# A four-layer graph attention stack: layers 1 and 3 start their first pass on eight source tiles with a maximum of their own, and rescale the sums later

## The reference, cut to what matters

```python
h = max(layernorm(x), 0)
Wh = h @ W;  s1 = Wh @ a1;  s2 = Wh @ a2
e = leaky_relu(s1[:, None] + s2[None, :], 0.2)
att = softmax(where(adj > 0, e, -big), axis=1)
x = x + activation(att @ Wh)     # elu, gelu in layer 1
```

## Time and profile before

| | |
|---|---|
| median of 3 runs | 751.4 us (751.36 to 753.15) |
| profiled execution | 751.58 us, its span 749.9 us |
| PE busy | 739.0 us, 99%, 6504 records |
| DVE busy | 624.9 us, 83% |
| ACT busy | 327.3 us, 44% |
| granted clock | 0.999 over the span |

### The profile page before, as it was taken

The page is one execution under the profiler, slowest core; times in us unless marked ns, Lnnn a source line. Parts: engine busy times, 40 slices in busy tenths (PEclk is TensorE's granted clock), DMA queues, the critical chain, the costliest instruction groups (busy, mean ns, idle before and its releaser), DMA issues.

```text
span 749.9 us, 16133 instructions
## 1 busy us (share of the span) xinstructions
PE 739.0 (99%) x6504; PEld 731.6 (98%) x6504; DVE 624.9 (83%) x1061; ACT 327.3 (44%) x899; POOL 16.6 (2%) x38
## 2 busy tenths in 40 slices
PE   9999999999999999999999999999999999999998
PEld 9899999999999999999999999999989989998998
DVE  5999879797797968879796797969887969797987
ACT  4978432462443336134353414534450362546230
POOL 4000000000000000000000000000000000000000
PEclk9999999999999999999999999999999999999999
DMA  9991000000000000000000000000000000000011
GB/s 294 370 386 78 30 29 1 28 0 28 28 0 28 0 28 0 28 28 0 28 0 28 28 0 28 0 0 1 30 2 1 1 29 2 1 1 29 2 29 29
DMA packets 14370, 30.98 MB, mean 41 GB/s; under 512 B 1384, under 2 KB 7680, under 8 KB 14336
## 3 DMA queue, kind: packets, MB, share of 16 engines
q1 hardware_dynamic: 11648, 21.58, 8.1%
q0 software_dynamic: 2688, 8.92, 3.5%
HBM read 29.37 MB, written 1.13 MB: 41 GB/s over the span
## 4 chain that ended last, share of the span: by engine, by line
PE 92%; DVE 3%; ACT 3%; issue 1%; POOL 0%; DVEq 0%; POOLq 0%
PE acc L514 55%; PE acc L552 24%; PE side L657 3%; PE side L458 3%; ACT adjT L805 1%; DVE probs L1433 1%; PE acc L479 1%; PE acc L607 1%; ACT V L838 1%; PE acc L437 1%; PE side L622 0%; DVE stats L1538 0%; PE side L577 0%; PE side L591 0%; PE side L489 0%
## 5 line engine op out<-in xcount | busy, mean ns | idle before, releaser
L514 PE MATMUL acc<-V,probs 128*128 128x129 f32 x3840 | 436.8, 275 | 2.0 <-DVE probs L1334 1.5
L514 PEld LDWEIGHTS acc<-V,probs 128*128 128x128 f32 x3840 | 432.7, 192 | 2.9 <-DVE V L1278 1.6
L1342 DVE SCALAR_TENSOR_TENSOR probs<-rho,t_now,adjT 128x1024 f32<-128x1024 f32 x238 | 289.9, 1277 | 10.5 <-PE acc L514 8.5
L1433 DVE SCALAR_TENSOR_TENSOR probs<-rho,t_now,adjT 128x640 f32<-128x640 f32 (+4 forms) x185 | 148.3, 857 | 15.0 <-PE acc L552 11.8
L906 ACT ACTIVATE hpT<-rows 32x256 f32<-32x256 f32 x224 | 92.8, 414 | 66.6 <-DVE rows L1379 64.2
L552 PE MATMUL acc<-stage,probs 128*128 128x129 f32 x1024 | 116.9, 275 | 0.1
L552 PEld LDWEIGHTS acc<-stage,probs 128*128 128x128 f32 x1024 | 115.4, 192 | 0.8 <-issue 0.5
L552 PE MATMUL acc<-V,probs 128*128 128x129 f32 x768 | 90.6, 276 | 0.4 <-DVE probs L1433 0.3
L552 PEld LDWEIGHTS acc<-V,probs 128*128 128x128 f32 x768 | 88.0, 192 | 1.0 <-DVE probs L1433 0.5
L891 ACT ACTIVATE fill<-mean_now,empty 128x128 f32<-128x128 f32 x120 | 36.7, 395 | 92.4 <-DVE den L1355 92.3
L1387 DVE TENSOR_TENSOR X<-X,side 128x512 f32<-128x512 f32 x28 | 19.3, 688 | 63.5 <-PE side L657 63.5
(11 more groups left out here) (213 smaller groups left out, 407.6 us busy)
## 6 DMA issues: line engine op xcount, KB each, us to landing
stage<-in_adj_t_dram SPq DMA_DIRECT2D x24, 512.0 KB, 8.0
rho<-rho_dram POOLq DMA_DIRECT2D x15, 512.0 KB, 3.9
hpT<-in_adj_t_dram SPq DMA_DIRECT2D x4, 512.0 KB, 8.7
xn<-in_adj_t_dram SPq DMA_DIRECT2D x4, 512.0 KB, 9.2
rho<-s_dram SPq DMA_DIRECT2D x3, 512.0 KB, 3.8
X<-in_x_dram SPq DMA_DIRECT2D x2, 512.0 KB, 4.4
W0t<-in_W_t_dram SPq DMA_DIRECT2D x1, 512.0 KB, 5.2
W<-in_L_gnn_W_heads_dram SPq DMA_DIRECT2D x1, 512.0 KB, 6.5
```

The costliest lines, as they stand in the source:

```text
L514: last = nc.tensor.matmul(group(c, k), probs[:, j % RING, k * P:(k + 1) * P], V[:, j, :], start=(j == 0 and k % PER_BANK == 0), stop=(j == ...
L1342: nc.vector.scalar_tensor_tensor(probs[:, j % RING, :], rho[:, c * CH:(c + 1) * CH], t_now[:, j:j + 1], adjT[:, j, c * CH:(c + 1) * CH], A ...
L1433: return nc.vector.scalar_tensor_tensor(slot_of(n, p, j)[:, first:end], rho[:, at + first:at + end], t_now[:, j:j + 1], adjT[:, j, at + fi ...
```

## The change

In layers 1 and 3 (`EARLY`) the first pass is cut in two. For source tiles 0 to 7, whose scores exist since pass 2 of the layer before, a maximum of their own is taken (`early_maximum`, spread by PE in `spread_early_max`, `early_center`). t, v and rho of their own are made (`early_factors`, `early_rho`, into a new buffer `rho_early`), V is scaled with them (`scale_early_v`), and the eight tiles of pass 0 are spread through the hole, on DVE and on PE. When the true maximum is there, ACT multiplies the sums in PSUM by a factor for each target, one bank after another (`rescale`), and then the tiles 8 to 15 are added. For passes 1 to 3 V of tiles 0 to 7 is brought to the true maximum by one more multiplication. The `keep_warm` calls of these two holes go, `late_s1` moves behind tiles 10 and 11 of pass 0, the mean of layer 3 moves to pass 1, and layer 2 keeps its form but for the order of `late_s1`.

The diff below goes from PE's order to ACT's (`factors_after_early`) and to DVE's (from `tiles(0, 2, 9, 16)` on), here for layer 1. DVE's order for layer 3 is the same in kind: the tiles 0, 1, 2 and 3 to 4 stand behind the statistics of chunk 2, behind its norm, behind the norm of chunk 3, and behind `take_scores` and `late_scale`.

```diff
+    EARLY = (1, 3)
-        spare_bank, max_bank = acc[:, 0, 2, 0:2 * P], acc[:, 0, 2, 2 * P:3 * P]
+        spare_bank, max_bank, early_bank = side[:, 0, 0:P], side[:, 0, P:2 * P], acc[:, 0, 2, 2 * P:3 * P]
+            def early_unit(n, asides):
+                for j in range(NK - 2):
+                    early_tile(n, j, range(NK))
+                    if j in asides:
+                        asides[j]()
+                for ks in banks_of():
+                    for j in (NK - 2, NK - 1):
+                        last = early_tile(n, j, ks)
+                    if ks[-1] < NK - 1:
+                        last.then_inc(early_summed, 1)
+            def rest_of_first_pass(n, asides):
+                for b, ks in enumerate(banks_of()):
+                    pe.wait_ge(rescaled, NB * (early_no(n) - 1) + b + 1)
+                    if b == 0:
+                        pe.wait_ge(late_v_ready, late_v_no(n, NK))
+                    for j in (NK, NK + 1):
+                        pe.wait_ge(probs_ready, probs_no(n, 0, j) + 1)
+                        early_tile(n, j, ks)
...
+            def spread_early_max(n):
+                pe.wait_ge(early_max_ready, early_no(n))
+                nc.tensor.matmul(early_bank, early_max[:, 0:1].to_broadcast([P, P]), ident_neg[:, :],
+                                 start=True, stop=True).then_inc(early_maxT_psum, 1)
-            def rest_of_scores(n):
...
+            def first_layer_scores():
+                project_rows(2, 0)
+                early_unit(1, {
+                    0: lambda: (transpose_normed(1, 1, 0, x_written, chunk_no(1, 1, 0)),
+                                transpose_normed(1, 1, 1, x_written, chunk_no(1, 1, 1))),
+                    1: lambda: (late_wh(1, 1, 0), transpose_rows(3, 0, hT_ready, chunk_no(1, 1, 0)), late_wh(1, 1, 1),
+                                transpose_normed(1, 2, 0, x_written, chunk_no(1, 2, 0))),
+                    2: lambda: (project_rows(3, 0), late_wh(1, 2, 0)),
+                    3: lambda: transpose_normed(1, 3, 0, x_written, chunk_no(1, 3, 0)),
+                    4: lambda: (late_wh(1, 3, 0), spread_late_max(1))})
+            def third_layer_scores():
+                early_unit(3, {
+                    0: lambda: (transpose_normed(3, 1, 1, hT_ready, chunk_no(3, 0, 1)), late_wh(3, 1, 0)),
+                    1: lambda: (late_wh(3, 1, 1), transpose_normed(3, 2, 0, x_written, chunk_no(3, 2, 0))),
+                    2: lambda: (late_wh(3, 2, 0), transpose_normed(3, 3, 0, x_written, chunk_no(3, 3, 0))),
+                    3: lambda: late_wh(3, 3, 0),
+                    4: lambda: spread_late_max(3)})
...
-                             (11, 1): lambda: rows_of_s1(1)})
+                             (11, 1): lambda: rows_of_s1(1),
+                             (13, 1): lambda: spread_early_max(1)})
...
+                    rest_of_first_pass(1, {10: lambda: late_s1(1, 3), 11: lambda: late_s1(1, 2)})
...
+                    rest_of_first_pass(3, {10: lambda: late_s1(3, 3), 11: lambda: late_s1(3, 2), 14: lambda: sum_raw(3)})
...
-                        late_unit(n, 2, {(0, 1): half[1], (4, 0): half[2], (6, 0): half[3], (13, 1): lambda: rows_of_s1(m)})
-                        late_unit(n, 3, {})
+                        late_unit(n, 2, {(0, 1): half[1], (4, 0): half[2], (6, 0): half[3], (10, 1): lambda: rows_of_s1(m),
+                                         (12, 1): lambda: spread_early_max(m)})
+                        late_unit(n, 3, {(14, 1): five[0]})
...
+                    late_unit(3, 1, {(1, 1): lambda: mean_rows(3, WL[:, 2, 0:D], 1, late_rho_ready, 12)})
...
+            def factors_after_early(n):
...
+                late_rho(n, 0)
+                late_rho(n, 1)
+                act.wait_ge(factor_ready, e)
+                rescale(n, 0)
+                act.wait_ge(late_vexp_ready, n)
+                scale_late_v(n, 8, 12)
+                rescale(n, 1)
+                rescale(n, 2)
+                scale_late_v(n, 12, 16)
+                nc.scalar.activation(v[:, 0:NK, :], v[:, 0:NK, :], ACT.Copy, scale=shift[:, 1:2]).then_inc(v_rescaled, 1)
+                late_rho(n, 3)
+                late_rho(n, 2)
...
-            tiles(0, 2, 9, 16)
-            take_scores(1, 0)
+            tiles(0, 2, 9, 13)
+            early_maximum(1)
+            tiles(0, 2, 13, 16)
+            early_center(1)
             add_to_x(1, 1, 0)
             add_to_x(1, 1, 1)
             late_statistics(1, 1)
             late_denominators(1, 2)
             late_divide(1, 2, 0)
             late_scale(1, 1)
             late_elu_rows(2, 0)
             late_norm(1, 1)
+            tiles(1, 0, 0, 1)
             late_denominators(1, 3)
             late_divide(1, 3, 0)
             add_to_x(1, 2, 0)
             late_elu_rows(3, 0)
+            tiles(1, 0, 1, 2)
             late_statistics(1, 2)
             late_norm(1, 2)
+            tiles(1, 0, 2, 3)
             add_to_x(1, 3, 0)
             late_statistics(1, 3)
             late_norm(1, 3)
+            tiles(1, 0, 3, 4)
             take_scores(1, 1)
             late_scale(1, 2)
+            tiles(1, 0, 4, 5)
...
                 take_scores(n, 2)
+                if n in EARLY:
+                    tiles(n, 0, 5, 6)
+                    late_center(n)
+                    tiles(n, 0, 6, 7)
+                    rescale_factors(n)
+                    late_vy(n)
+                    tiles(n, 0, 7, 16)
+                    tiles(n, 1, 0, 6)
+                    if n > 1:
+                        mean(n, n)
...
-                    tiles(3, 1, 8, 13)
+                    tiles(3, 1, 8, 10)
+                    mean_elu(3)
+                    tiles(3, 1, 10, 13)
+                    add_fill(3)
                     add_linear(4, 0, 0)
                     add_to_x(4, 0, 0)
                     tiles(3, 1, 13, 14)
```

More of the change, by code:

```diff
@@ L527, in last_bank_read, with banks_of, early_tile @@
                     pe.wait_ge(late_rows, rows_no(n, p, i))
+            def banks_of():
+                return [range(b * PER_BANK, min((b + 1) * PER_BANK, NK)) for b in range(NB)]
+            def early_tile(n, j, ks):
+                if j in (0, 1, 4) and ks[0] == 0:
+                    pe.wait_ge(early_v_ready, 3 * early_no(n) - 2 + (0, 1, 4).index(j))
+                if j < NK:
+                    pe.wait_ge(probs_ready, probs_no(n, 0, j) + 1)
+                for k in ks:
+                    last = nc.tensor.matmul(late_group(0, k), slot_of(n, 0, j)[:, k * P:(k + 1) * P], V_of[n % 2][:, j, :],
+                                            start=(j == 0 and opens_bank(0, k)), stop=(j == NT - 1), skip_group_check=True)
+                if ks[-1] == NK - 1:
+                    last.then_inc(summed, 1)
+                return last
+            def early_unit(n, asides):
[14 more added lines that the diff above has]
+                    for j in (NK, NK + 1):
+                        pe.wait_ge(probs_ready, probs_no(n, 0, j) + 1)
+                        early_tile(n, j, ks)
+                for j in range(NK + 2, NT):
+                    if j == 12:
+                        pe.wait_ge(late_v_ready, late_v_no(n, j))
+                    pe.wait_ge(probs_ready, probs_no(n, 0, j) + 1)
+                    early_tile(n, j, range(NK))
+                    if j in asides:
+                        asides[j]()
             def late_unit(n, p, asides):
@@ L748, in rest_of_scores, with second_layer_scores @@
+            def second_layer_scores():
+                late_wh(2, 1, 0)
+                late_wh(2, 1, 1)
+                late_wh(2, 2, 0)
                 keep_warm(1, spare_idle)
-                late_wh(n, 3, 0)
+                transpose_normed(2, 3, 0, x_written, chunk_no(2, 3, 0))
                 keep_warm(1, spare_idle)
-                spread_late_max(n)
-                late_s1(n, 2)
-                late_s1(n, 3)
+                late_wh(2, 3, 0)
+                keep_warm(1, spare_idle)
+                spread_late_max(2)
+                late_s1(2, 3)
+                late_s1(2, 2)
@@ new lines, in early_rho, with scale_early_v @@
+            def early_rho(n):
+                act.wait_ge(s1_in, 16 * n)
+                for k in range(2):
+                    at = slice(512 * k, 512 * k + 512)
+                    nc.scalar.activation(rho_early[:, at], rho[:, at], ACT.Exp, bias=neg_e[:, 0:1],
+                                         scale=-(1 - ALPHA)).then_inc(early_rho_ready, 1)
+                act.wait_ge(early_vexp_ready, early_no(n))
+            def scale_early_v(n, first, end):
+                v = V_of[n % 2]
+                for t in range(first, end):
+                    last = nc.scalar.activation(v[:, t, 0:D], v[:, t, 0:D], ACT.Copy, scale=v[:, t, D:D + 1])
+                last.then_inc(early_v_ready, 1)
@@ L1432, in late_probs @@
                 at = tiles_of(p)[0] * P
+                if n in EARLY and p == 0 and j < NK:
```

(9 more changed lines are left out.)

196 lines of the change are left out of this document (137 added, 59 removed).

## The result

The changed kernel takes 759.47 us (median of four executions; 758.69 to 760.21), the kernel before 751.38 (median of four as well): ratio 1.0103, 95% interval 1.0083 to 1.0123. It is **slower by 1.0%**. 758.2 was forecast. The profiled execution took 758.93, with a span of 757.3 (749.9 before).

A forecast was written before the change was run, and what follows sets the result against it. PE, busy 99%, was taken as the bound, with 8.1 us freeable. Layer 1 +4.1, layer 3 −0.9, its end +3.6 make 6.8 on 751.58, 758.4; the median, 0.2 lower, 758.2 us (own range 755.5 to 761).

The forecast's parts named there:

- (A): Layer 1's hole: DVE waits in early_center for the spread early maximum, so PE waits 2.1 us before transpose_rows(2, 0).
- (B): Layer 1: PE waits 0.45 us for early tile 0, behind early_rho's load and exponentials, and 0.45 for tile 1.
- (C): Layer 1: tile 3 stands behind add_to_x(1, 3, 0) on DVE, which needs project_rows(3, 0) from PE: 2.25 us waiting.
- (D): Layer 1, behind early tile 4: PE waits for the maximum to spread and for tile 5, behind DVE's scores: 1.8 us.
- (E): Layer 1: DVE has late_center, tile 6, factors and vy ahead of early tile 7, so PE waits 0.75 us.
- (F): Layer 1: PE waits 0.1 us for ACT's rescaling of the PSUM sums; the range was 0 to 0.8 for each layer.
- layer 3 until pass 1: Layer 3 before its pass 1: waits of 3.25 us against 4.1 freed, so 0.9 us faster.
- layer 3's passes 1 to 3: End of layer 3: the moved mean delays nonlinear_late(4, 0) to 10.8 us into pass 1; PE loses 3.6 us.
- the rival of the clock: Both holes: PE's clock falls during the new waits with keep_warm gone, 3 us more, 761.2 us; chance 0.05.
- the cover at the end: Rival, end of layer 3: ACT's and DVE's lead survives the moved mean, 3.6 us less, 754.6 us; chance 0.15.
- The hole was not filled: The rival had DVE's new tiles filling its idle time in the holes, only (D) staying: 745.5 us; chance 0.12.
- The waits did not come to half: The rival halved the 15 us of waits counted in the holes and at the end: no change, 751 us; chance 0.08.

The follow-up runs named there:

- Experiments 3 and 4: Changed kernel with layer 1's early_center behind late_statistics (early_factors later too): 758.68 us; then also rows_of_s1(1) behind tile 8 instead of 11 of pass 2: 757.60 us.
- all_orders: Changed kernel with all order repairs together: ACT's order at layer 3's end, early_center, rows_of_s1 and early tiles moved, nothing left out: 748.67 us, ratio 0.9961.
- center_rows: Changed kernel with early_center(1) and early_factors(1) later and rows_of_s1(1) three tiles of pass 2 earlier: 757.60 us, ratio 1.0094.
- mean_in_pass0: all_orders with layer 3's mean moved back into pass 0 (sum_raw behind tile 12, mean_rows behind tile 14): 747.15 us, ratio 0.9942.
- best: mean_in_pass0 with rows_of_s1(3) one tile earlier in layer 2's pass 2, behind tile 9: 747.18 us, ratio 0.9943.
- light_tiles: Changed kernel with DVE writing only 512 of 1024 columns of early tiles 0 to 7 in layers 1 and 3: 753.58 us, ratio 1.0025.

## Why the prediction was right, step by step

The sum came out nearly as forecast, 6.8 against 7.35 us between the profiled executions (751.58 to 758.93), and so did the terms and the places of the waits. Lost time of PE, forecast and read from PE's timelines:

| step | forecast | measured |
|---|---|---|
| (A) line 647 behind the early maximum | 2.1 | 1.75 |
| (B) tile 0, tile 1 | 0.45, 0.45 | 0.4, 0.4 |
| (C) tile 3 behind `add_to_x(1, 3, 0)` | 2.25 | 2.2 |
| (D) spread of the maximum and tile 5 | 1.8 | 0.6 + 1.0 |
| (E) tile 7 | 0.75 | 0.8 |
| (F) rescaling, banks | 0.1 | 0.2 |
| layer 1 in all, freed time taken off | +4.1 | +3.8 |
| layer 3: pass 3 of layer 2 later; tiles 0, 1, 3, 6 and 7; rescaling | 0.75; 2.4; 0.1 | 0.75; 2.7; 0.2 |
| layer 3 until pass 1, freed time taken off | −0.9 | −0.3 |
| layer 3's passes 1 to 3 | +3.6 | +3.8, the moved `mean_rows` (0.2) included |

Some luck is in the sum, since the misses of layers 1 and 3 (0.3 too much, 0.6 too little) partly cancel. What was off:

- (A) is 0.35 smaller. `add_to_x` started at 537.25, not 537.4, and elu followed denominators that no longer waited. The size was right only as a wait, not as a price. Experiments 3 and 4 show that removing (A) alone gives 0.1 to 0.2, since the load of rho (ACT could use it at 540.57) is due at the same moment. The prediction priced both (0.45 in (B)) but did not say that they cover each other.
- Layer 3 before pass 1 gained 0.3 instead of 0.9. Tile 0 lost 0.7 instead of 0.45: DVE's first early tile also waited 0.4 us for PE to free a ring slot, which the walk left out. Tile 1 lost 0.3 instead of 0.2, and the rescaling 0.2 instead of 0.1.
- In (B) the working doesn't give its term: tile 0 wanted at 543.95 and ready at 544.25 is 0.3, not 0.45. The trace shows 0.4 (543.84 less 543.44), so the term came out closer than its working. In the rival of the clock, work that takes 3 us at full clock would cost 3 us more in each of the two layers at half of it, 6 in all and not 3, so its 761.2 should have been 764.2.
- The measured terms of layer 1 add up to 7.35. With 0.2 for the spread and 4.0 taken off that is 3.6, where the timeline shows 3.8. The rest lies behind the waits, where the first records cost a little more: 16 records of tile 0 take 1.86 (543.84 to 545.70), not 1.79.
- (F): the rescaling from PSUM to PSUM starts every 0.26 us (three from 564.75, the next instruction at 565.52), like the scalings of V behind it (0.25, also read from PSUM). That is the lower end of the range, and PE lost 0.2 all the same. By the experiment without the multiplications only 0.1 of that hangs on them. The lines, of ACT in the changed kernel:

```profile
564.75 0.86 ACT L1229 ACTIVATE acc<-acc,factor 128x129 f32<-128x129 f32 x3 [1.82 <-PE acc L570]
565.52 1.15 ACT L1194 ACTIVATE stage<-acc,stage 128x128 f32<-128x128 f32 x4
```

The Trainium skill (ScalarE: Activation LUTs, "Step-by-step: what each stage is for") says that PSUM is the lower-latency destination for ACT. These rows don't show it: from PSUM, 0.26 us start to start into PSUM and 0.25 into SBUF. What differs is the source, as scalings from SBUF into SBUF start every 0.29 us ((2.15 − 0.39) / 6, with 0.39 for the length of the last one). (F) did not fall to 0 by it.

The rivals: the cover at the end did not hold (ACT at 45% busy, and late all the same). The hole was not filled: DVE's idle time was there (3.3 us at line 1703 alone) and could not be used, since the next tile stood behind that wait. The waits did not come to half: 14.7 us are measured in both layers and the end, of 14.75 counted. The clock did not fall: PEclk is at full in every slice of the page, with waits of 2 us and no `keep_warm` in these holes. The overall idea is sound. With the order repaired layers 1 and 3 each gain about 2 us, and the kernel is 0.6% faster than before.

## What to carry to other kernels

When work is spread into a hole, count for each queue what stands behind every wait, and put independent work ahead of the instruction that waits, not behind it: nearly the same instructions in another order were worth 12 us here (758.69 to 747.02 by the lowest values). An engine's busy share says nothing on this; ACT at 45% and DVE with 3 us of idle both held up PE. Where two things reach a step together, removing one shows nothing, so remove both before the first is called harmless. An order that is repaired can hold the same fault in a new place, as tile 1 of layer 1 did in `all_orders`.

## What was not expected of the hardware

Most executions of one and the same kernel fall on two values about 1.5 us apart (before: 751.07 to 751.60 and 752.75 to 753.15). One of `center_rows` lies 3.3 above the lowest, with a mean granted clock of 0.995. Two traces of kernels that are the same until layer 2, `mean_in_pass0` and `best`, show where. PE's timeline at the start, first of `mean_in_pass0`, then of `best`:

```profile
1.64 7.43 PE L509 MATMUL acc<-ident 128*128 128x128 f32 x40 [1.64 <-POOL ident L413]
8.90 0.95 PE L762 MATMUL acc<-a_sb,W0t 128*128 128x2 f32 x8
```

```profile
1.64 6.07 PE L509 MATMUL acc<-ident 128*128 128x128 f32 x40 [1.64 <-POOL ident L413]
8.69 1.05 PE L762 MATMUL acc<-a_sb,W0t 128*128 128x2 f32 x8 [0.98 <-DMA W0t<-in_W_t_dram]
```

The 40 records of `keep_warm` took 7.43 us in the one and 6.07 in the other, where PE was through at 7.7 and stood idle for 0.98 us until the weights came. Windows of PE behind this (length, busy and records, granted clock, DMA share, GB/s), again first of `mean_in_pass0`, then of `best`:

```profile
12.00:14.00 2.00, 2.00 (x19) 1.00 1.04 359
```

```profile
10.00:12.00 2.00, 2.00 (x18) 0.83 1.04 397
12.00:14.00 2.00, 2.00 (x11) 0.50 1.03 357
14.00:16.00 2.00, 2.00 (x16) 0.82 1.03 350
```

In `best` the clock stands at 0.50, its lower level of 1.2 GHz, in the stretch of 12 to 14 us, where 11 records fall instead of 19. The program is 1.6 us behind from there on (20.29 and 21.85 for the first `probs` matmul of layer 0). Ahead of the fall PE's work differs in two things, the faster 40 records and the idle 0.98 us behind them. Idle time by itself is not enough: in the traces of `center_rows` and `light_tiles` PE idles 0.33 and 0.34 us at the same place, with the 40 records in 6.74 and 6.56, and the clock stays at 1.00, as it does in the changed kernel's holes with waits of 2 us. Neither the cause of the fall nor why the same 40 records took 6.07 to 7.68 us in the traces at hand is shown. A difference below 1.5 us between medians of four executions is therefore not a finding here by itself.
